# Cross-attention in a decoder layer on one core: scores by head in 32-row tiles, exponents by ScalarE from PSUM, keys split 128 + 128 + 52

## The reference, cut to what matters

```python
Q = (query @ Wq.T).reshape(B, T_q, 16, 32)
K = (context @ Wk.T).reshape(B, 77, 16, 32)
V = (context @ Wv.T).reshape(B, 77, 16, 32)
scores = einsum('bqhd,bkhd->bhqk', Q, K) / sqrt(32)
attn = softmax(scores, axis=-1)
out = einsum('bhqk,bkhd->bqhd', attn, V).reshape(B, T_q, 512) @ Wo.T
```

## Time and profile before

| | |
|---|---|
| median of 3 runs | 2475.74 us (2470.34 to 2476.79) |
| the profiled execution | 2468.48 us |
| its span, first to last instruction | 2466.4 us |
| TensorE (PE) busy | 2373.7 us, 96% |
| VectorE (DVE) | 1171.2 us, 47% |
| ScalarE (ACT) | 943.5 us, 38% |
| GpSimd (POOL) | 466.5 us, 19% |
| mean DMA rate | 57 GB/s |

### The profile page before, as it was taken

How to read it: one execution, slowest core, us unless ns; L and a number is a source line. 1 busy time by engine, 2 the same in 40 slices (tenths; PEclk the granted TensorE clock), 3 DMA queues, 4 the chain that set the end, 5 groups by cost and what they waited for, 6 DMA issues and landing times.

```text
span 2466.4 us, 32984 instructions
## 1 busy us (share of the span) xinstructions
PE 2373.7 (96%) x11592; PEld 1960.9 (80%) x11592; DVE 1171.2 (47%) x1977; ACT 943.5 (38%) x1504; POOL 466.5 (19%) x554
## 2 busy tenths in 40 slices
PE   8778799999999999999999999999999999999999
PEld 4777578888888887788888888888888888888887
DVE  5999688888888887532222212222222212212211
ACT  3997445444444443433223222223222222323321
POOL 3787222222222222111001001101101101101100
PEclk9988899999999999999999999999999999999999
DMA  9554601101111112400000000000010010000000
GB/s 344 173 186 174 217 1 69 44 34 68 44 53 49 39 52 69 162 1 35 34 15 19 34 19 15 34 34 0 34 34 0 34 34 0 34 34 0 34 17 17
DMA packets 83116, 141.23 MB, mean 57 GB/s; under 512 B 18023, under 2 KB 18535, under 8 KB 82663
## 3 DMA queue, kind: packets, MB, share of 16 engines
q1 hardware_dynamic: 83072, 140.68, 16.4%
HBM read 79.42 MB, written 61.24 MB: 57 GB/s over the span
## 4 chain that ended last, share of the span: by engine, by line
PE 89%; DVE 4%; ACT 3%; POOL 2%; issue 2%; DMA 1%; ACTq 0%; POOLq 0%; SPq 0%; DVEq 0%
PE ps L360 77%; PE ps L1503 5%; PE ps L1483 2%; POOL xu L639 1%; PE ps L1397 1%; ACT tu L770 1%; ACT tu L771 1%; PE ps L1333 1%; PE ps L1416 1%; PE ps L1359 1%; POOL yd L633 0%; DVE ql L1018 0%; DVE xt L1018 0%; DVE es L1196 0%; DVE rmax L1194 0%
## 5 line engine op out<-in xcount | busy, mean ns | idle before, releaser
L1018 DVE TENSOR_TENSOR gtl<-ps,gth 128x512 fp32r<-128x512 f32 x256 | 177.1, 692 | 1089.1 <-ACT gth L907 1089.1
L360 PE MATMUL ps<-xt,wuh 128*128 (+1 forms) x2048 | 638.5, 393 | 5.0 <-DVE xt L1018 4.9
L905 ACT ACTIVATE ps<-ps,up_b 128x512 f32<-128x512 f32 x256 | 169.5, 662 | 990.5 <-PE ps L360 990.5
L360 PEld LDWEIGHTS ps<-xt,wuh 128*128 128x128 f32 x2048 | 383.6, 188 | 93.5 <-DVE xt L1018 8.9
L360 PE MATMUL ps<-wdl,gth 128*128 128x512 f32 x1024 | 402.2, 393 | 0.0
L360 PE MATMUL ps<-wdh,gtl 128*128 128x512 f32 x1024 | 402.1, 393 | 0.0
L360 PE MATMUL ps<-wdh,gth 128*128 128x512 f32 x1024 | 402.0, 393 | 0.0
L360 PE MATMUL ps<-xt,wul 128*128 (+1 forms) x1024 | 400.7, 391 | 0.0
L608 POOL TENSOR_TENSOR rstd<-var_e,mhalf 128x4 f32<-128x4 f32 x48 | 53.2, 1109 | 1300.3 <-DVE var_e L1007 1300.3
L669 POOL TENSOR_TENSOR es<-es,rinv 128x308 f32<-128x308 f32 x256 | 170.9, 699 | 446.3 <-DVE rinv L1207 446.3
L360 PEld LDWEIGHTS ps<-wdh,gth 128*128 128x128 f32 x1024 | 192.2, 188 | 44.1
(11 more groups left out here) (186 smaller groups left out, 3753.5 us busy)
## 6 DMA issues: line engine op xcount, KB each, us to landing
x<-x_scratch SPq DMA_DIRECT2D x32, 1024.0 KB, 5.6
xa<-in_x SPq DMA_DIRECT2D x16, 1024.0 KB, 5.4
x_scratch<-xa SPq DMA_DIRECT2D x16, 1024.0 KB, 4.3
x_scratch<-x SPq DMA_DIRECT2D x16, 1024.0 KB, 4.3
out_x<-x SPq DMA_DIRECT2D x16, 1024.0 KB, 4.3
xu<-in_wexpT SPq DMA_DIRECT2D x4, 1024.0 KB, 18.5
yd<-in_wcon SPq DMA_DIRECT2D x4, 1024.0 KB, 9.9
wd_scratch<-fold SPq DMA_DIRECT2D x4, 1024.0 KB, 6.9
```

The lines of the kernel that those rows point to most:

```text
L360: mm = pe.matmul(bank, a, b, start=first and i == 0, stop=last and i == n - 1)
L905: A(bank, bank, ACT.Gelu, bias=up_b[:, m:m + 1]).then_inc(act_gelu, 1)
L1018: sub = lambda o, a, b: V.tensor_tensor(o, a, b.bitcast(F32), ALU.subtract)
```

## The change

Scores: kh and kl hold 78 columns (77 keys and one of padding) per chunk, each head's keys in its own 32 rows. scores(t) has 48 matmuls of 32 rows, 128 stationary columns and 78 moving columns: for each chunk and each of the three products, four heads one after another, head h in rows 32h to 32h+31 and into bank h. The factor 1/sqrt(32) goes into wqh and wql.

Softmax: shift only takes the maxima, negated, in two instructions of two banks each. ScalarE computes the exponents straight from the score banks, one ACTIVATE for each head and chunk (16 for a tile, 77 elements each), with the negated maximum as its bias and the sum as a second output. scores(t) now waits until all exponents of the tile before it are done. sums(t) has the reciprocal alone and waits for all 16 exponents. The exponents of tiles 1 and 3 are spread between the copies in ScalarE's order; values(0) is ahead of scores(1) on TensorE.

Keys: the 308 columns of a chunk are pieces of 128, 128 and 66 (52 keys and 14 columns that are zero). High and low part of the third piece stand in one tile pt2, rows 0 to 51 and 64 to 115, and vh and vl have the last 52 rows twice, so values(f) has eight matmuls. pt2 is zeroed once by GpSimd at the start of attention (p_zero). The rounds are all written out. load_k has two transfers, load_v fourteen.

```diff
-    KP = (CK + 2) // 3
-    CKP = 3 * KP
-    NJ = KC * 3
-    V_AT = [0, 2 * HD, 5 * HD, 9 * HD]
+    LP = L + L % 2
+    KT = CK - 2 * P
+    KB = P // 2
+    KU = KB + 2
+    CKP = 2 * P + KU
+    VW = [2 * HD, HPC * HD, HPC * HD]
+    V_AT = [0, VW[0], VW[0] + VW[1], sum(VW)]
...
         def attn_loop(eng, body):
             inside = lambda g: lambda d: 0 <= g + d < NG
-            for g in (0, 1):
-                body(g, inside(g))
-            with eng.Fori(2, NG - 2) as g:
-                body(g, lambda d: True)
-            for g in range(NG - 2, NG + 2):
+            for g in range(NG + 2):
                 body(g, inside(g))
...
             def load_k(b):
                 for hl, t in ((0, kh), (1, kl)):
-                    for h in range(HPC):
-                        sp.dma_start(raw(t[h * HD:(h + 1) * HD, b % 2, :, h * L:(h + 1) * L]),
-                                     kt_d[hl, h * HD:(h + 1) * HD, :, b * L:(b + 1) * L]).then_inc(k_loaded, 16)
+                    sp.dma_start(raw(t[:, b % 2, :, 0:L]), kt_d[hl, :, :, b * L:(b + 1) * L]).then_inc(k_loaded, 16)
...
             pool.wait_ge(v_zero, 1)
+            for j in (2, 3):
+                pool.wait_ge(fold_stored[j], 16 * 2)
+            nc.gpsimd.memset(pt2[:, :, :].bitcast(F32), 0.0).then_inc(p_zero, 1)
...
-                def exp(t):
-                    if has(0):
-                        act.wait_ge(e_ready, T * g + t + 1)
-                        e = es[t % 2][:, :, 0:CK]
-                        A(e, e, ACT.Exp, scale=SCALE).then_inc(exp_done, 1)
+                def exp(t, heads):
+                    if not has(0):
+                        return
+                    for h in heads:
+                        if h % 2 == 0:
+                            act.wait_ge(top_ready, 2 * (T * g + t) + h // 2 + 1)
+                        for f in range(KC):
+                            at, j = h * KC + f, f * HPC + h
+                            e = A(es[t % 2][:, f, h * L:(h + 1) * L], ps[:, h, f * LP:f * LP + L], ACT.Exp,
+                                  bias=rmax[:, t % 2, at:at + 1], accum_out=rsum[:, t % 2, j:j + 1])
+                        e.then_inc(exp_ps, 1)
...
-                exp(0)
+                exp(0, (0, 1, 2, 3))
                 if has(1) and not (isinstance(g, int) and g == 0):
                     apply2(g + 1)
                 hi_v(0)
                 hi_x(0)
-                exp(1)
+                if not (isinstance(g, int) and g == 0):
+                    exp(1, (0, 1))
                 hi_v(1)
                 hi_x(1)
+                if isinstance(g, int) and g == 0:
+                    exp(1, (0, 1))
+                exp(1, (2,))
                 hi_v(2)
+                exp(1, (3,))
                 hi_v(3)
...
                 hi_p(0, 0)
                 hi_x(2)
-                exp(2)
+                exp(2, (0, 1, 2, 3))
                 hi_x(3)
                 hi_p(1, 0)
-                exp(3)
-                for o in range(KC):
+                exp(3, (0, 1))
+                hi_q(0)
+                exp(3, (2, 3))
+                for o in range(1, KC):
                     hi_q(o)
...
                     dve.wait_ge(s_done, n + 1)
-                    V.tensor_reduce(mx, sc, AX.X, ALU.max).then_inc(max_step, 1)
-                    dve.wait_ge(max_step, n + 1)
-                    V.tensor_tensor(es[t % 2][:, :, 0:CK].rearrange("p f (h k) -> p f h k", k=L), sc,
-                                    mx.unsqueeze(3).broadcast_to([P, KC, HPC, L]), ALU.subtract).then_inc(e_ready, 1)
+                    for h in (slice(0, 2), slice(2, 4)):
+                        V.tensor_reduce(mx[:, h], sc[:, h], AX.X, ALU.max, negate=True).then_inc(top_ready, 1)
...
-                    dve.wait_ge(exp_done, n + 1)
-                    V.tensor_reduce(rsum[:, t % 2, :].rearrange("p (f h) -> p f h", f=KC),
-                                    es[t % 2][:, :, 0:CK].rearrange("p f (h k) -> p f h k", k=L), AX.X, ALU.add).then_inc(sum_step, 1)
-                    dve.wait_ge(sum_step, n + 1)
+                    dve.wait_ge(exp_ps, HPC * n + HPC)
                     V.reciprocal(rinv[:, t % 2, :], rsum[:, t % 2, :]).then_inc(rinv_ready, 1)
...
-                    after(pe, e_ready, T * g + t)
+                    after(pe, exp_ps, HPC * (T * g + t))
                     tok = slice(t * P, (t + 1) * P)
                     b = (g // GB) % 2
                     for f in range(KC):
-                        mm = split3(pe, ps[:, f, 0:CK], [(qh[:, f, tok], ql[:, f, tok], kh[:, b, f, :], kl[:, b, f, :])])
+                        cols = slice(f * LP, (f + 1) * LP)
+                        for i, (q, k) in enumerate(((qh, kh), (qh, kl), (ql, kh))):
+                            for h in range(HPC):
+                                at = slice(h * HD, (h + 1) * HD)
+                                mm = pe.matmul(ps[:, h, cols], q[at, f, tok], k[at, b, f, :], start=(i == 0), stop=(i == 2))
                     mm.then_inc(s_done, 1)
...
-                            f, c = divmod(4 * q + j, 3)
-                            mm = pe.transpose(b[0:KP, j * P:(j + 1) * P], es[t % 2][:, f, c * KP:(c + 1) * KP], ident[:, :])
+                            keys = es[t % 2][:, j, q * P:min(q * P + P, CKP)]
+                            mm = pe.transpose(b[0:keys.shape[1], j * P:(j + 1) * P], keys, ident[:, :])
...
-                    passes = [(c, v, pt) for c in (2, 1, 0) for v, pt in ((vh, pth), (vh, ptl), (vl, pth))]
+                    passes = [(c, v, pt[:, KC * c + f, :]) for c in (1, 0) for v, pt in ((vh, pth), (vh, ptl), (vl, pth))]
+                    passes[3:3] = [(2, v, pt2[:, f, :]) for v in (vh, vl)]
...
+                values(0)
                 if not start:
                     scores(1)
-                values(0)
```

More of the change, by code:

```diff
@@ L37, in decoder_layer @@
     CK = HPC * L
-    KP = (CK + 2) // 3
-    CKP = 3 * KP
-    NJ = KC * 3
-    V_AT = [0, 2 * HD, 5 * HD, 9 * HD]
+    LP = L + L % 2
[5 more added lines that the diff above has]
+    V_AT = [0, VW[0], VW[0] + VW[1], sum(VW)]
+    assert 2 * L <= P + L and 2 * P < CK <= 2 * P + KB
     MC = HID // P
@@ L173, in decoder_layer @@
     ql = r2.put("ql", [P, KC, GT], F32R)
-    kh = r2.put("kh", [P, 2, KC, CK], F32R)
-    kl = r2.put("kl", [P, 2, KC, CK], F32R)
+    kh = r2.put("kh", [P, 2, KC, LP], F32R)
+    kl = r2.put("kl", [P, 2, KC, LP], F32R)
+    r2.at += 4 * 4 * KC * (CK - LP)
     assert r2.at <= yd_at
@@ L178, in decoder_layer @@
     free_es1 = r2.at - 4 * KC * CKP
-    vh = r2.put("vh", [KP, KC, V_AT[3]], F32R)
-    vl = r2.put("vl", [KP, KC, V_AT[3]], F32R)
+    vh = r2.put("vh", [P, KC, V_AT[3]], F32R)
+    vl = r2.put("vl", [P, KC, V_AT[3]], F32R)
     free_last = r2.at
@@ L186, in decoder_layer @@
     free_values = r2.at
-    pth = r2.put("pth", [KP, NJ, GT], F32R)
-    ptl = r2.put("ptl", [KP, NJ, GT], F32R)
+    pth = r2.put("pth", [P, 2 * KC, GT], F32R)
+    ptl = r2.put("ptl", [P, 2 * KC, GT], F32R)
+    pt2 = r2.put("pt2", [P, KC, GT], F32R)
     free_last2 = r2.at
@@ L800, in _ @@
             act.wait_ge(wq_loaded, 16)
-            A(wqh[:, :, :], wq_raw[:, :, :], ACT.Copy).then_inc(wq_hi, 1)
+            A(wqh[:, :, :], wq_raw[:, :, :], ACT.Copy, scale=SCALE).then_inc(wq_hi, 1)
             for n in range(MC, 2 * MC, 2):
@@ L839, in hi @@
                     if len(out.shape) == 3:
-                        bank = bank[0:KP].rearrange("p (j n) -> p j n", j=4)
+                        bank = bank[0:out.shape[0]].rearrange("p (j n) -> p j n", j=4)
                     his.done(A(out, bank, ACT.Copy), hi_slot(n))
@@ L844, in hi_p @@
                     if has(d):
-                        for q in range(3):
-                            hi(pth[:, 4 * q:4 * q + 4, t * P:(t + 1) * P], P_SLOT[t] + q)
+                        for q, part in ((0, pth[:, 0:KC]), (1, pth[:, KC:2 * KC]), (2, pt2[0:KT])):
+                            hi(part[:, :, t * P:(t + 1) * P], P_SLOT[t] + q)
                 def hi_x(c):
@@ L1164, in lo_p @@
                     if has(d):
-                        for q in range(3):
-                            part = lambda w: w[:, 4 * q:4 * q + 4, t * P:(t + 1) * P]
-                            lo(part(ptl), part(pth), P_SLOT[t] + q)
+                        for q, part, high in ((0, ptl[:, 0:KC], pth[:, 0:KC]), (1, ptl[:, KC:2 * KC], pth[:, KC:2 * KC]),
+                                              (2, pt2[KB:KB + KT], pt2[0:KT])):
+                            tok = slice(t * P, (t + 1) * P)
+                            lo(part[:, :, tok], high[:, :, tok], P_SLOT[t] + q)
                 def lo_x(c):
```

29 lines of the change are left out of this document (16 added, 13 removed).

## The result

The changed kernel takes **2559.75 us** (median of 4 runs, 2556.11 to 2560.41), the kernel before 2473.04 us (4 runs, 2469.92 to 2476.79): a ratio of 1.0348, 95% interval 1.0335 to 1.036. The forecast was 2555 us, slower. The profiled execution has a span of 2558.2 us and took 2560.0 us.

The account below looks back on a forecast made before the run. TensorE bounds the 44.4 us round; 43.2 us of work plus 6.2 of waits gives 49.4, +80 us in 16 groups. 2468.5 + 80 = 2548.5, plus 7.3 to the median: 2555 us, range 2448 to 2700.

Parts of the forecast that it names:

- The three places of the wait: TensorE waits in a round: 1.6 us at scores(1), 1.1 at turn_x(0), 2.5 at turn_p(0).
- hand-made layout: Four engines' orders on one time axis with estimated durations and every wait: 49.4 us a round against 44.4.
- 6.2 us of waits: TensorE's waits per round, added to 43.2 us of its work for a round of 49.4 us.
- a clock that falls makes all slow cases a little worse: TensorE's granted clock, 0.81 in the first round with waits of 2 to 4 us; no size given.
- Scores: Row-tiled score block on TensorE: 1.70 us as now, loads hidden, streams in turn; effect zero, range -0.7 to +3.6 a tile.
- one step per foursome: Scores on TensorE: four matmuls go together at 0.11 us, so 12 x 0.11 = 1.32 us a block.
- rival 1: Row-tile loads go one after another: scores 5.28 us, 62.6 us a round, about 2765 us; chance 0.12.
- Exponents: ScalarE's 16 instructions of 77 elements: 0.33 us each (0.21 to 0.44), 5.3 us a tile against 1.24.
- Values: Eight matmuls for nine on TensorE, 0.23 us each: 0.93 us less a round, sure and on the path.
- VectorE "is worth nothing by itself": Freeing VectorE of subtraction and sum gains nothing: it was 6 us short of the round and waits for ScalarE.
- Zeroing of pt2: GpSimd at the start of attention, ahead of its first multiplication: at most 2 us, once.
- Writing out: Written-out attention rounds fetch more instructions: 0, with up to 1 us a round if fetching can't keep up.

Follow-up runs that it names:

- sums after first low: Changed kernel with the earlier softmax and TensorE order, pt2 zeroed later, addresses shifted 640 bytes, VectorE's sums(0) between lo_v(0) and lo_x(0), sums(1) after lo_x(1): 2460.92 us.
- sum by vector: Changed kernel with pt2 zeroed behind round 0's reciprocal root, exponents on ScalarE without the sum output, and VectorE summing them: 2567.39 us, ratio 1.0381 to the kernel before.
- pieces only: Kernel before with only the key pieces of 128, 128 and 52 (eight matmuls in values, pt2); loop, scores and softmax kept: 2472.74 us, ratio 1.0001.
- Sum by vector, lo first: As sum by vector, with VectorE's sums(1) moved behind all four low parts of the values: 2513.53 us, ratio 1.0162 to the kernel before.
- softmax as before: Changed kernel with pt2 zeroed later and one exponent instruction per tile, VectorE again doing maximum, subtraction and sum; TensorE's new order kept: 2492.36 us, ratio 1.0077.

## Why the prediction was right, and where it wasn't

**The forecast held**: slower, 2555 us against 2559.75, by its mechanism, and 79.0 us in the 15 rounds, 5.3 us each, where it had 5.0 us a round. The three places of the wait are those it named. With time 0 at the end of scores(0) (639.76 in the chain), the hand-made layout put the end of exp(0) at 7.2 us and the trace has it at 7.0; the start of turn_x(0) at 10.0, and it was 9.9; that of turn_p(0) at 19.1, and it was 20.2.

**But its 6.2 us of waits were 3.3**, and the rest came from a term it didn't have. That the two sums agree so well (49.4 forecast, 49.5 measured) is luck. Taking the 43.3 us of sums after first low for TensorE's work with no waits, the second kind of round is 50.0 - 43.3 = 6.7 us longer. The waits are 1.0 + 1.3 + 1.0 = 3.3, for 1.6 + 1.1 + 2.5 and 1.0 of small ones in the forecast. At half the clock turn_x(0) took 1.11 us for 0.44, values(1) 3.41 for 1.86, turn_x(1) 0.85 for 0.44, values(2) 2.11 for 1.86: **2.9 us**. That leaves 0.5 us that isn't put down to anything. In the first kind, 48.9 us, the waits are the same 3.3 us and the stretch at half the clock is 3.4 us long, all of it work, so it costs 1.7; 0.6 us are left. The forecast had seen the clock of 0.81 in the first round and wrote that "a clock that falls makes all slow cases a little worse"; it gave it no price. It fell out even because a slower TensorE comes later to turn_p(0), where it would have waited anyway: the layout had it ready at 16.6, it was at 19.2. A wait of 2.5 us became one of 1.0, and turn_p(0) began 1.1 us later than the layout said. In the first kind of round it began at 19.1 us (590.85 to 609.97), as in the layout.

**Scores.** Taken as 1.70 us, nearest to the row of the instruction that is replaced; measured 1.47, or about 1.65 with what the block behind loses. The forecast's other bound (one step per foursome, 1.32 us) was the nearer one for the block alone, and rival 1 (loads one after another) fell. "Loads hide behind the other rows' streams while the streams go in turn" is the wrong picture: the four loads and the four matmuls start together, and a foursome steps by 0.11 us, as one pair does in the earlier trace rows. What sets that step no run here separates.

**Exponents.** Taken as 0.33 us, measured 0.30, of which 0.10 is the accumulator (0.21 without it, in sum by vector). The forecast's own term without any sum was too large (0.33 for 0.21), and its price for the sum, "nothing, or at most another smallest instruction", was right at the upper end (0.10 for 0.11). Two errors that cancel in part. From the figures of the Trainium skill ("ScalarE: Activation LUTs", What ACT_TABLE_LOAD costs) the estimate for a pointer bias and 77 elements is 0.25 us; the measurement is 0.21 and decides.

**Values.** 0.93 us a round by 0.23 us a matmul: in sums after first low 0.9. Right, and "on the path" was right only as long as TensorE is the bound. In pieces only, 0.2 came out.

**VectorE "is worth nothing by itself".** True of the 10 us that it was freed of. But its order is worth a great deal: 26 us for two low parts moved ahead of the reciprocal, 54 us where the sum stands there too. The forecast had lo_v(1) behind sums(1) as its largest wait and was right to; the expectation of sum by vector then forgot it. Part of both figures is the clock, as shown there.

**Zeroing of pt2: "at most 2 us, once".** This step failed. It priced the zeroing (1.80 us) in front of GpSimd's first multiplication and left out the wait for a transfer ahead of it, and what else stood behind it on GpSimd's queue, the reciprocal root. It cost 6.2 us in the traces, 6.8 us between the medians.

**Memory layout** was not in the prediction. Of the 4.1 us behind the last mark one shift of the addresses gave back 2.4; that the rest is of the same kind is not shown. **Writing out** at 0 was right.

What the parts are worth per round, from pairs of kernels that differ in one: exponents on ScalarE, 49.5 - 45.25 = +4.2 us with TensorE's new order and 54.0 - 43.75 = +10.3 with the old; that order, 45.25 - 43.75 = +1.5 with VectorE's softmax and 49.5 - 54.0 = -4.5 with ScalarE's; row tiles with written-out rounds, 43.75 - 44.25 = -0.5; pieces, -0.2; the order of VectorE's sums, -0.4. They don't add up one by one, and that is the lesson: the value of a part depends on the order around it. Not tried: whether ScalarE's exponents with a whole new order of all engines come under 43.3 us. Sum by vector, lo first, is the nearest to it: 45.8 us in the rounds with a clock of 1.00, 47.35 in those at 0.96.

## What to carry to other kernels

Price moved work by its place in each engine's fixed order: list what stands behind it, and who waits for that. A sum of busy time (36 of 49 us here) says nothing of it. The same holds for a wait that is added: here the wait and 1.8 us of zeroing cost 6.2 us, because a short instruction that others needed was queued behind them. And when the bound's own work shrinks, lay out the next engine before booking the gain: here 0.4 of 1.1 us stayed hidden (43.75 for 43.33) until two VectorE sums had moved. Last, give a wait of the bound engine two prices: its length, and what the clock takes behind it.

## What was unexpected of the hardware

- The sum of an ACTIVATE is an instruction of its own in the trace, and costs 0.10 us a piece (steps of 0.30 and 0.21 us).
- With waits of 1.0 and 1.3 us and 1.5 us of work between them goes a stretch at a granted clock of 0.50, from within the second wait or its end, 3.4 us long in one round and 6.7 us in the next; the rest of the round has 1.00. It costs 1.7 and 2.9 us for 3.3 us of waiting. Two waits of 0.7 us (softmax as before) left the clock at 1.00. In the first round of the changed kernel the clock was 0.57, for 0.81.
- A foursome of 32-row loads and matmuls of 78 columns takes the 0.11 us of one pair, and the return to full height some 0.15 to 0.2 us.
- With the buffers at other addresses the same matmuls of the feed-forward stage take 91.0 us a group, or 90.7 and 90.8 in turn: 2.4 us over 14 groups.
